# Decoder layer on one core: the end of the last attention batch tile by tile, weight splits rescheduled, three of them on GpSimd

## What is computed

```
x = layernorm(x + attention(x))          # 4 batches x 256 tokens x 256, 16 heads of 16, causal softmax
x = layernorm(x + gated_mlp(x, ctx[e]))  # e by token id, 4 experts of 256 x 256
x = layernorm(x + moe(x))                # e = argmax of a router; gate, up (256 x 1024), silu, down; times the router's weight
```

## Time and profile before

| | |
|---|---|
| median of 3 runs | 321.23 us (320.64 to 323.58) |
| the profiled execution | 322.61 us, its span 320.8 us |
| busy: TensorE, VectorE, ScalarE, GpSimd | 248.8, 185.1, 130.3, 73.9 us |
| attention | from 0 to 139.8 us of the span, when the last scatter lands |
| second stage | 139.8 to 202.9 us |
| third stage | 202.9 us to the end |

### The profile page before, as it was taken

One profiled execution on the slowest core, in us unless ns is written; L12 is line 12 of the kernel. 1 busy time (PEld: TensorE's weight loads), 2 busy tenths in 40 slices (PEclk: granted clock), 3 DMA queues, 4 the chain that ended last, 5 costly groups with the idle time before them and its releaser, 6 DMA issues.

```text
span 320.8 us, 5861 instructions
## 1 busy us (share of the span) xinstructions
PE 248.8 (78%) x1991; PEld 165.2 (52%) x1992; DVE 185.1 (58%) x406; ACT 130.3 (41%) x218; POOL 73.9 (23%) x125
## 2 busy tenths in 40 slices
PE   4795789887986773447797537679999999999990
PEld 3364556555664551124676432236666656666570
DVE  3868577776889447813776758023544445455441
ACT  4451565855946674305575300033323213333210
POOL 8400000100141303810333268100222111222222
PEclk9799699999999998596999556599999999999997
DMA  6999072422253741448200011240000000000000
GB/s 201 339 326 284 6 261 68 127 73 67 68 164 84 215 133 39 191 144 298 102 3 0 2 42 68 89 115 2 16 18 1 2 11 16 16 16 16 9 13 2
DMA packets 18055, 29.29 MB, mean 91 GB/s; under 512 B 2796, under 2 KB 13550, under 8 KB 18032
## 3 DMA queue, kind: packets, MB, share of 16 engines
q1 hardware_dynamic: 16592, 25.81, 26.4%
q0 software_dynamic: 1440, 3.17, 2.7%
HBM read 19.69 MB, written 10.03 MB: 93 GB/s over the span
## 4 chain that ended last, share of the span: by engine, by line
PE 54%; DVE 16%; issue 9%; ACT 7%; DMA 5%; POOL 5%; SPq 3%; POOLq 0%; ACTq 0%; DVEq 0%
PE ps L1103 34%; DVE arena L848 3%; PE ps L1408 3%; ACT wf_hi L480 3%; PE ps L1213 2%; PE ps L1174 2%; PE ps L1109 2%; POOL sorted L422 2%; POOL sorted L451 2%; SPq L335 2%; DMA ring<-wqkvT 1%; PE ps L1170 1%; DVE wf_lo L686 1%; DVE arena L845 1%; DMA arena<-Wf 1%
## 5 line engine op out<-in xcount | busy, mean ns | idle before, releaser
L1103 PE MATMUL ps<-wf_hi,arena 128*128 x336 | 82.0, 329 | 2.8 <-DVE arena L1031 1.6
L1103 PE MATMUL ps<-wf_lo,arena 128*128 x168 | 55.2, 328 | 0.0
L1103 PEld LDWEIGHTS ps<-wf_hi,arena 128*128 128x128 f16 x336 | 32.8, 98 | 26.8 <-issue 6.7
L639 ACT ACTIVATE arena<-ps 128x512 f32<-128x512 f32 x22 | 13.2, 598 | 65.3 <-PE ps L1103 65.3
L1031 DVE SCALAR_TENSOR_TENSOR arena<-ps,arena 128x512 f32<-128x512 f32 x22 | 15.2, 692 | 25.3 <-ACT arena L639 13.5
L1109 PE MATMUL ps<-wf_hi,ones 128*128 128x512 f16 x51 | 18.9, 545 | 12.4 <-issue 6.1
L686 DVE SCALAR_TENSOR_TENSOR wf_lo<-ring,wf_hi 128x1024 f16<-128x1024 f32 x17 | 20.5, 1219 | 8.6 <-ACT wf_hi L480 8.6
L1103 PE MATMUL ps<-xT_hi,arena 128*128 x88 | 20.3, 295 | 5.4 <-DVE arena L991 4.6
L1103 PEld LDWEIGHTS ps<-wf_lo,arena 128*128 128x128 f16 x168 | 16.4, 98 | 9.4
L1103 PE MATMUL ps<-arena,xT_hi 128*128 128x512 f16 (+1 forms) x64 | 17.2, 358 | 4.9 <-DVE arena L805 2.3
L457 POOL TENSOR_SCALAR veps<-mv 128x1 f32<-128x1 f32 x11 | 2.5, 226 | 79.6 <-DVE mv L1051 79.6
(11 more groups left out here) (202 smaller groups left out, 525.6 us busy)
## 6 DMA issues: line engine op xcount, KB each, us to landing
ring<-Wf SPq DMA_DIRECT2D x17, 512.0 KB, 3.8
sorted<-fill SPq DMA_DIRECT2D x1, 4515.0 KB, 22.0
arena<-Wf SPq DMA_DIRECT2D x7, 512.0 KB, 6.0
arena<-sorted SPq DMA_DIRECT2D x22, 129.0 KB, 2.1
sorted<-fill SPq DMA_DIRECT2D x1, 1419.0 KB, 7.2
ring<-xT SPq DMA_DIRECT2D x4, 256.0 KB, 5.5
X<-x_tok SPq DMA_DIRECT2D x1, 1024.0 KB, 8.4
ring<-ctxT SPq DMA_DIRECT2D x2, 512.0 KB, 3.9
```

The costliest lines, as they stand in the source:

```text
L639: a.activation(sg[:, half * 512:(half + 1) * 512], ps[:, 2 * half, :], ACT.Silu, scale=1 / W_SCALE).then_inc(sg3, 1)
L1103: last = t.matmul(dst, xs(k), ws(k), start=(k == 0 and m == 0), stop=(k == nk - 1 and m == 2))
```

## The change

- At steps 5, 9 and 13 (g = 1) the two pieces of `maxima` and the two calls of `outputs` alternate on VectorE, where there are maxima left.
- `scores` and `maxima` of step 15 move from step 10 to step 9 (`EARLY`), with them `max_T(3)` and the four DMAs of `max_rows(3)`.
- A table gives how many chunks a step splits: none at steps 0, 5, 8 and 9, two at 11, 12 and 14, one at the others. Where it is two, the second chunk's high half (chunks 8, 10 and 13) is made by GpSimd (`split_hi` with `tensor_scalar`, new L451): that of chunk 8 between `inv_std` and `scatter2` of batch 1, those of 10 and 13 behind this `scatter2`. VectorE waits for it on a semaphore of its own, `c_hi_g`. Loads follow the same table.
- `stats1(2)` moves ahead of `outputs(3, .)`; chunk 15 is split around `o_copy(15)`, its low half ahead of `outputs(3, 0)`.
- For the last batch, `out_T`, high and low half, `out_project`, residual, statistics, inverse deviation and normalization go tile by tile, with banks of their own (`LAST_T`, `LAST_O`). Chunk 16's low half stands ahead of the last residuals.
- The low halves of chunks 17 to 20 wait for `scat2_sent`, which GpSimd raises behind the last scatter's issue.
- `keep_warm` matmuls of TensorE: 4 ahead of the last projection, two behind every third expert number, 8 once the last tile is normalized, 4 once the scatters have landed; the 16 of before go.

```diff
+EARLY = STEPS - AHEAD - 2
+LAST_T, LAST_O = (7, 6), (1, 2)
...
+        ATT_LO = (0, 1, 1, 1, 1, 0, 1, 1, 0, 0, 1, 2, 2, 1, 2, 1)
...
+            def split_hi(n):
+                src, arrived, value = staged(n)
+                pool.wait_ge(arrived, value)
+                g.tensor_scalar(chunk_dst(ORDER[n], True), src, W_SCALE, None, ALU.mult).then_inc(c_hi_g, 1)
+
             for b in range(B - 2):
                 pool.wait_ge(mv1, TB * (b + 1))
                 inv_std(mv[:, :, 1], TB, rs1)
+                if b == B - 3:
+                    split_hi(BY_POOL[0])
                 scatter2(b)
+            for n in BY_POOL[1:]:
+                split_hi(n)
...
-            pool.wait_ge(mv1, NT)
-            inv_std(mv[:, :, 1], TB, rs1)
+            for j in range(TB):
+                tt = NT - TB + j
+                pool.wait_ge(mv1, tt + 1)
+                link(g.tensor_scalar(veps[:, j:j + 1], mv[:, j, 1:2], EPS, None, ALU.add))
+                g.tensor_tensor(rstd[:, j:j + 1], veps[:, j:j + 1], minus_half[:, 0:1], ALU.pow).then_inc(rs1, 1)
             scatter2(B - 1)
+            g.memset(veps[:, :], 0.0).then_inc(scat2_sent, 1)
...
                 if b >= 1 and g == 1:
                     outputs(b - 1, 0)
-                    outputs(b - 1, 1)
-                if step + AHEAD < STEPS:
+                    if step + AHEAD < STEPS:
+                        maxima(*divmod(step + AHEAD, NG), between=lambda: outputs(b - 1, 1))
+                    else:
+                        outputs(b - 1, 1)
...
+                if step == EARLY:
+                    maxima(B - 1, NG - 1)
+                    max_T(B - 1)
...
-                if 1 <= step < STEPS - 1 and n < ATT_CHUNKS:
+                for _ in range(ATT_LO[step]):
                     split_lo(n)
                     n += 1
...
+            split_lo(n)
+            n += 1
             outputs(B - 1, 0)
             outputs(B - 1, 1)
-            stats1(B - 2)
             norm1(B - 2)
-            o_lo(B - 1)
+            for j in range(TB):
+                dve.wait_ge(oT_hi_last, j + 1)
...
             split_lo(n)
             n += 1
-            residual(B - 1)
-            stats1(B - 1)
-            norm1(B - 1)
+            last_residual(0)
+            last_mean(0)
+            last_residual(1)
+            last_mean(1)
...
+            dve.wait_ge(scat2_sent, 1)
             while n < NCH - LAST:
                 split_lo(n)
                 n += 1
```

More of the change, by code:

```diff
@@ L212, in build @@
         lg_sb, ex_rdy, w_rdy, row_rdy = (sem(n) for n in ("lg_sb", "ex_rdy", "w_rdy", "row_rdy"))
+        oT_last, oT_hi_last, oT_lo_last, scat2_sent = (sem(n) for n in ("oT_last", "oT_hi_last", "oT_lo_last", "scat2_sent"))
         endT, end_hi, end_lo = sem("endT"), sem("end_hi"), sem("end_lo")
@@ L255, in build, with hi_wait @@
         xTv_lo = xT_lo[:, :].rearrange("p (k t) -> p k t", k=NK)
-        ATT_CHUNKS = NCH - LATE - RING
+        ATT_LO = (0, 1, 1, 1, 1, 0, 1, 1, 0, 0, 1, 2, 2, 1, 2, 1)
+        ATT_CHUNKS = sum(ATT_LO)
+        RING_CHUNKS = NCH - LATE
+        assert len(ATT_LO) == STEPS and RING_CHUNKS <= NCTX + (E - 1) * (EW // CH)
+        BY_POOL = tuple(sum(ATT_LO[:step]) + 1 for step in range(STEPS) if ATT_LO[step] == 2)
+        def hi_wait(engine, n):
+            behind = sum(c <= n for c in BY_POOL)
+            if n in BY_POOL:
+                engine.wait_ge(c_hi_g, behind)
+            else:
+                engine.wait_ge(c_hi, n + 1 - behind)
         CTX_AT = 8
@@ L321, in _ @@
             max_rows(0)
-            n = 0
+            n = used = 0
             for step in range(STEPS):
-                if step % NG == NG - 2 and step + 2 < STEPS:
+                if step % NG == NG - 2 and step + NG + 2 < STEPS:
                     max_rows(step // NG + 1)
-                while n < min(step + RING, NCH - LATE):
+                elif step == EARLY:
+                    max_rows(B - 1)
+                used += ATT_LO[step]
+                while n < min(used + RING, RING_CHUNKS):
                     load(n)
@@ L567, in _ @@
                     q_odds(stacked_at(step))
-                if step >= 1 and n < ATT_CHUNKS:
-                    split_hi(n)
+                for _ in range(ATT_LO[step]):
+                    if n not in BY_POOL:
+                        split_hi(n)
                     n += 1
@@ L573, in _ @@
             o_copy(STEPS - 2)
+            split_hi(n)
+            n += 1
             o_copy(STEPS - 1)
-            o_hi(B - 1)
+            for j in range(TB):
+                act.wait_ge(oT_last, j + 1)
+                a.activation(OT_hi[:, j], ps[:, LAST_T[j], 0:D].rearrange("p (k t) -> p k t", k=NK),
+                             ACT.Copy).then_inc(oT_hi_last, 1)
             def exps_router(part):
@@ L836, in stacks, with maxima @@
                               ).then_inc(q_even, 1)
-            def maxima(b, g):
+            def maxima(b, g, between=None):
                 n = NG * b + g
@@ L846, in maxima @@
                                 AX.X, ALU.max, negate=True).then_inc(maxed, 1)
+                if between is not None:
+                    between()
                 dve.wait_ge(s_rdy, 2 * n + 2)
@@ L1286, in _ @@
                     scores_T(0, 1)
-                if step + AHEAD < STEPS:
+                if step + AHEAD < STEPS and step != EARLY + 1:
                     scores(*divmod(step + AHEAD, NG))
@@ L1294, in _ @@
                     out_T(b - 1)
+                if step == EARLY:
+                    scores(B - 1, NG - 1)
                 if b >= 1 and g == 3:
```

61 lines of the change are left out of this document (51 added, 10 removed).

## The result

The changed kernel takes **323.06 us** (median of 20 runs, 320.85 to 326.1) against 321.5 us before (20 runs, 318.25 to 323.85): the ratio is **1.0046**, its 95% interval 1.0027 to 1.0065. Forecast was 320.4. So the kernel is not a little faster but half a per cent slower: a change with a dozen parts, of which, as will be seen, one takes back all that the others give. The profiled execution, 326.10 us with a span of 324.3, is the slowest of the 20 and 3.0 above the median. Ratios leave out executions over 1.5% above the fastest of the same kernel, among them this one, five of the eight with 46 warming matmuls, and two of 626.57 and 1337.64 us (chunk 8 on ScalarE; half the columns).

What follows compares the result with a forecast made beforehand. Bound by the chain of waits to the last scatter's landing: 126.0 + 9.6 + 3.4 = 139.0 against 139.79, 0.8 gained. The profiled 322.61 becomes 321.8, less 1.4 to the median 320.4 us; range 315.8 to 325.3, the forecast's own 318.4 to 323.

Steps and rivals of the forecast that it cites:

- the size of GpSimd's high half: Steps 11 to 13: each half takes 1.1 us, near the memset; over 2 us would show the prediction wrong.
- rival 2: GpSimd's high half takes much longer than a memset, 2.0 us of path per us; 324.5 from about 3.1; chance 0.15.
- Steps 5 to 9: Without chunks at steps 5 and 8, VectorE's statistics of batch 1 end at 99.7 instead of 103.02, 3.3 us earlier.
- Statistics to the outputs of batch 2: Steps 11 to 13: GpSimd enters the path; 10.9 us from batch 1's statistics, outputs at 110.6, 2.6 later than before.
- The clock: TensorE's clock falls to the 1.2 GHz level at 111, behind one long wait, costing 1.6 us on the path.
- Step 15: Residual, statistics and two low halves on VectorE ahead of batch 3's outputs make these another 1.6 us late, at 126.0.
- The earlier maxima: Step 12: rows of maxima arrive ahead of need, exponentials start 5.7 us earlier, but this gain is off the path.
- The tail: From batch 3's outputs to the last scatter's start: 9.6 us instead of 16.9.
- The stall: Scatter of 6.15 us at 130.66, held up by VectorE's six low halves; its removal gives 5.2 us.
- Landing: Last scatter takes 3.4 us to land, instead of 2.68, with loads of chunks 19 and 20 in flight.
- TensorE's late warming: Ahead of the second stage, until about 140 to 142: hidden by a weight load, costed at nothing, without cover up to 0.8.
- Rival 1: GpSimd's halves hold the path less or the clock stays up: 317.3, or 314.7 if batch 2's outputs aren't late; chance 0.28.

Runs made afterwards that it cites:

- 46 warming matmuls: Changed kernel plus 46 warming matmuls on TensorE in its wait at step 13, ahead of batch 2's second transposes: 323.78 us, ratio 0.9928 from three of eight executions.
- chunk 8 on ScalarE: Changed kernel with chunk 8's high half made by ScalarE, those of chunks 10 and 13 still by GpSimd: 320.17 us, ratio 0.9938.
- half the columns: Changed kernel with GpSimd making only columns 0 to 511 of its three high halves, ScalarE the others: 320.93 us, ratio 0.9958.
- the hold alone: Kernel before, with only the low halves behind the last normalization made to wait until the last scatter is issued: 318.93 us, ratio 0.9902.
- 57 warming matmuls: Changed kernel plus 57 warming matmuls on TensorE in its wait at step 13, ahead of batch 2's second transposes: 321.75 us, ratio 0.9982.
- 313.48: Changed kernel with only chunk 13's high half on GpSimd, those of chunks 8 and 10 on ScalarE: 313.48 us, ratio 0.974.
- the one of 310.87: Changed kernel with only chunk 13's high half on GpSimd and three VectorE low halves moved behind what they held up: 310.87 us, ratio 0.9619.
- the tail alone: Changed kernel with one chunk at each of steps 1 to 15, no early maxima, no alternation, nothing on GpSimd: 316.06 us, ratio 0.9805.

## Why the prediction was wrong, point by point

**The failed step is the size of GpSimd's high half.** The prediction took 1.1 us for it, "near the memset", with 2.1 as the upper bound; it takes 2.80 both times that VectorE waits for it, and 3.17 for chunk 13, with VectorE's low half and outputs beside it. The prediction had itself named a half of over 2 us as a sign of being wrong. The memset reads nothing and converts nothing. But rows of before in which GpSimd does read would have misled in the same way. Its affine selects (they keep or replace elements by position, without a conversion) took 0.64 us for 128x512 and 0.29 for 128x128, in float32 too, which is 0.9 ns for a column and 1.1 us for 1024. Whether the conversion or the operation makes 2.5 ns of it, no run separates. VectorE's 1.2 us, called its "same instruction", is the low half, another operation on another engine. The half counts twice on the path, so its error is 2 x 1.7 = 3.4 us, and the prediction's own sum with 2.80 gives 323.8, against 323.06 measured. That the two are 0.7 apart is in part luck, for other terms were off too: at the outputs of batch 3 the trace is 2.0 later than forecast (128.03 for 126.0), 3.4 from the halves less 1.0 from steps 5 to 9 and smaller ones. It is the mechanism of rival 2, at a size between its marks of 1.5 (gain gone) and 3.1 (over 1% slower), which the text gave 0.15; the order of both streams, the double count and the place were right. The affine select, in GpSimd's timeline of the kernel before:

```profile
4.72 0.64 POOL L391 TENSOR_SCALAR_AFFINE_SELECT maskS<-maskS 128x512 bf16<-128x512 bf16 x1
```

The Trainium skill (GPSIMD Engine Reference, section 3.1) has 1.03 cycles per element for up to two operations, by which an estimate is 0.9 us here; it has 2.6 cycles for an instruction with two inputs, by which an estimate is 2.2 us. This trace differs from both: 2.5 ns per column are 3 cycles at the 1.2 GHz of that page, for one input with a conversion to float16.

The other steps:

- **Steps 5 to 9**: gain 3.3 expected, 4.3 in the trace (98.71 for 103.02).
- **Statistics to the outputs of batch 2**: 10.9 expected, 14.17 measured. By parts: `inv_std` 2.10 (2.0), high half to low half 2.84 (1.15), low half 1.14 (1.15), normalization and scatters 4.12 (4.3), high half 2.83 (1.15), low half 1.14 (1.15). Only the two halves are off.
- **The clock**: 1.6 expected; 1.5 in the traces, 1.3 in the medians, 2.1 by the ratios. Right.
- **Step 15**: 1.6 late expected. The outputs of batch 3 are 7.8 late in all, 4.9 and 1.5 of it are from above, so 1.4. Right.
- **The earlier maxima are off the path**: right as the kernel stands. Without GpSimd's halves, too, table and maxima together give 0.5 at most, since a fallen clock and two high halves of ScalarE at step 14 take them.
- **The tail**: 9.6 expected, 9.71 measured. The stall's share of 5.2 is shown by the hold alone (6.15 to 1.07). Its price in the kernel is less, 3.2, since the low halves it delays have little room before the second stage.
- **Landing**: 3.4 taken, 4.71 in the profiled execution, which is 3.0 above its median; 2.9 to 3.5 in the profiles of all the experiments (without GpSimd's halves 128.22 to 131.28, 3.1). The term was right.
- **TensorE's late warming**: costed at nothing, "without that cover up to 0.8". In the profiled execution it had ended at 143.6, and TensorE waited 0.99 us for the first tile at 144.62, in the execution whose scatter landed after 4.71. With a landing after 2.9 to 3.1 the warming was in the chain of waits (57 warming matmuls, half the columns, chunk 8 on ScalarE). It held the first transpose up by an estimated 0.3 to 1.5 us there, the transpose's start less the landing and less 2.1. So the cover was thinner than the prediction had it.

Rival 1 had 314.7 for the case that the outputs of batch 2 aren't late at all. The kernel without GpSimd's halves goes further, with these outputs 4.6 us early (103.43 for 107.99), and yet takes 315.59. So rival 1's time is nearly met by luck: the 4.6 us are mostly lost again, to a clock that fell behind 2.90 us, to two high halves of ScalarE at step 14 and to the late warming. What chose between forecast and rival 2 was one duration that the trace of before didn't have.

## What to carry to other kernels

Work moved to an idle engine is paid by who waits for it, not by that engine's share: the same 2.80 us half cost nothing for chunk 13 and, for chunks 8 and 10, with the scatters queued between them, the low half and the clock behind them, the 9.6 us between 323.06 and 313.48. Before trusting such a move, look for a row of the same engine with the same inputs and conversion, and if there is none take several times the nearest one as upper bound: here the half took 2.6 times what the nearest rows gave. An engine whose instructions hold up another's (a row of low halves beside a scatter) is cheaper held for 3 us than left running, as long as what is held back has room afterwards. Before reading where a change loses its time, compare the profiled execution with the median: here 3.0 us of its span, a late landing among them, were its own.

## What the runs showed of the hardware

- GpSimd's `tensor_scalar` from float32 to float16 takes 2.80 us for 128x1024 and 1.52 for 128x512, and 3.17 and 3.26 (chunk 13 in the changed kernel and in the one of 310.87) for 128x1024 with VectorE at work beside it. Its affine select of 128x512 bfloat16, without a conversion, took 0.64 in the kernel before. VectorE's low half of the same size, with two inputs, takes 1.23, ScalarE's high half 1.05.
- A scatter of GpSimd takes 1.07 with VectorE silent, 1.62 with one low half beside it, 2.74 with two (without GpSimd's halves, at 101.71) and 6.15 in the row of six. The Trainium skill (SBUF — State Buffer, on the two sides) lets the loser of the shared port pair wait for a whole instruction, and with a two-input instruction of VectorE only where the GpSimd operation reads SBUF; in the trace it waits through several that follow each other closely. With one low half and with two it ends 0.95 after the last of them (106.66 and 103.51), the length of a whole undisturbed scatter; with six in a row about as long after the fifth. Not every row does this: in the kernel before, three scatters beside a row of five low halves (193.69 to 199.45) took 1.25, 1.97 and 1.97, the last of them in the earlier trace rows. What makes the difference is not shown.
- It goes the other way too: the low half of 1.23 took 2.06 with a GpSimd half beside it. And GpSimd's power of two columns took 1.56 with low halves beside it, 0.73 without.
- TensorE's granted clock fell to 0.50, the level of 1.2 GHz, behind waits of 2.90 us (no GpSimd half) and of 2.50 (46 warming matmuls): the transposes there still took 0.63, the values 1.51. It fell behind the wait of 12.61 too. It stayed at 1.00 through 12.5 us of warming.
- Warming itself ran at half clock where TensorE came to it with gaps: 12 matmuls took 5.30 us, at 0.50 from 130 to 134 (no GpSimd half), against 3.88 with the tail alone.
